# Graph network kernel: the local pass multiplies full fp32 words, and VectorE makes the clamp in front of the inverse root

## What is computed

```python
def _gcn_conv(x, W, b, src, dst, dinv):
    h = x @ W
    norm = dinv[src] * dinv[dst]
    agg = jax.ops.segment_sum(h[src] * norm[:, None], dst, num_segments=x.shape[0])
    return agg + (dinv * dinv)[:, None] * h + b
x = _l2norm(_gcn_conv(node_embedding, W1, b1, ...))          # 128 -> 256
def f(z):
    z1 = _l2norm(_gcn_conv(z, Wf1, bf1, ...))                # 256 -> 256
    return _gcn_conv(z1, Wf2, bf2, ...) + z
k1 = f(x); k2 = f(x + 0.5 * k1); k3 = f(x + 0.5 * k2); k4 = f(x + k3)
x = x + (k1 + 2.0 * k2 + 2.0 * k3 + k4) / 6.0
return _gcn_conv(x, W2, b2, ...)                             # 256 -> 128
x = _layernorm(x + that)
```

## Time and profile before

| | us |
|---|---|
| time before, median of 2 runs | 7419.17 (7414.28 to 7424.07) |
| span of the profiled execution | 7463.9 |
| PE busy in it | 6262.2 (84%) |
| DVE busy | 6114.0 (82%) |
| POOL busy | 4840.9 (65%) |
| ACT busy | 3838.3 (51%) |

### The profile page before, as it was taken

The page is one execution under the profiler, slowest core; times in us unless marked ns, Lnnn a source line. Parts: engine busy times, 40 slices in busy tenths (PEclk is TensorE's granted clock), DMA queues, the critical chain, the costliest instruction groups (busy, mean ns, idle before and its releaser), DMA issues. The chain is left out here.

```text
span 7463.9 us, 156875 instructions
## 1 busy us (share of the span) xinstructions
PE 6262.2 (84%) x37260; PEld 5197.7 (70%) x37260; DVE 6114.0 (82%) x15796; ACT 3838.3 (51%) x10696; POOL 4840.9 (65%) x5469
## 2 busy tenths in 40 slices
PE   7699889899999657989989998999888765877776
PEld 3588888888889436867766676667666554865664
DVE  8588778787888777889879977997799887878887
ACT  6466666666666576733661166116622233654443
POOL 0488888888873576855776577657744565546665
PEclk8799999999999899999999999999999998988998
DMA  0365555554444466879779977997799765543432
GB/s 2 102 165 161 161 160 158 162 161 152 146 145 152 146 190 199 247 257 297 229 223 332 329 226 224 331 327 228 230 385 387 259 186 151 152 138 119 125 123 86
DMA packets 981268, 1483.74 MB, mean 199 GB/s; under 512 B 156967, under 2 KB 450705, under 8 KB 980647
## 3 DMA queue, kind: packets, MB, share of 16 engines
q1 hardware_dynamic: 685479, 922.39, 37.2%
q0 software_dynamic: 141504, 309.42, 16.2%
q10 hardware_dynamic: 153664, 244.12, 9.0%
HBM read 902.58 MB, written 573.11 MB: 198 GB/s over the span
## 5 line engine op out<-in xcount | busy, mean ns | idle before, releaser
L1336 PE MATMUL bank<-c_rows,sums_all 128*128 128x256 f32 (+1 forms) x3920 | 1320.9, 420 | 550.5 <-DVE c_rows L1487 304.3
L751 PE MATMUL bank<-wf_w,c_xt 128*128 128x256 f32 x6272 | 1615.0, 381 | 2.0 <-DVE y L1545 2.0
L1381 ACT ACTIVATE c_xt<-bank 128x512 f32<-128x512 f32 (+1 forms) x980 | 556.8, 568 | 1586.6 <-issue 831.0
L1307 POOL DMA_INDIRECT c_rows<-t_tab,src_pair x784 | 870.2, 1110 | 705.6 <-PE bank L1336 546.2
L1336 PEld LDWEIGHTS bank<-c_rows,sums_all 128*128 128x128 f32 x3920 | 633.9, 194 | 984.7 <-DVE c_rows L1487 478.7
L751 PEld LDWEIGHTS bank<-wf_w,c_xt 128*128 128x128 f32 x6272 | 1133.7, 191 | 127.0 <-ACT c_xt L1381 3.5
L1487 DVE SCALAR_TENSOR_TENSOR c_rows<-bank,carry,c_rows 32x256 f32<-32x256 f32 (+1 forms) x1950 | 913.7, 469 | 274.3 <-PE bank L1336 117.6
L1307 POOL DMA_INDIRECT c_rows<-z_tab,src_pair x784 | 770.7, 983 | 293.3 <-issue 189.5
L1085 DVE TENSOR_TENSOR lx_lo<-bank,lx_hi 128x512 fp32r<-128x512 f32 (+1 forms) x1000 | 658.6, 659 | 260.6 <-ACT lx_hi L1030 217.4
L1030 ACT ACTIVATE lx_hi<-bank 128x512 fp32r<-128x512 f32 (+1 forms) x1000 | 569.4, 572 | 580.4 <-PE bank L999 418.6
L741 PE MATMUL bank<-wf_hi,lx_hi 128*128 128x256 f32 x3200 | 725.0, 309 | 62.7 <-issue 49.4
(11 more groups left out here) (333 smaller groups left out, 14629.2 us busy)
## 6 DMA issues: line engine op xcount, KB each, us to landing
c_z<-z_tab SPq DMA_DIRECT2D x882, 256.0 KB
z_tab<-lz SPq DMA_DIRECT2D x400, 256.0 KB
t_tab<-lt SPq DMA_DIRECT2D x400, 256.0 KB
z_tab<-y ACTq DMA_DIRECT2D x392, 256.0 KB
c_own<-z_tab SPq DMA_DIRECT2D x392, 256.0 KB
t_tab<-y ACTq DMA_DIRECT2D x392, 256.0 KB
c_own<-t_tab SPq DMA_DIRECT2D x392, 256.0 KB
fl_x<-x_tab SPq DMA_DIRECT2D x396, 128.0 KB
```

The source lines that it names most:

```text
L751: last = nc.tensor.matmul(out, x(k), w[:, k, :], start=(k == 0), stop=(k == ks - 1 and not bias))
L1307: pool.indirect_dma_start(out=rows[:, s, i, 0:win], out_offset=None, in_=source, in_offset=bass.IndirectOffsetOnAxis(ap=m["src_i"][:, t:t ...
L1336: nc.tensor.matmul(psum[s % 2][:, i * win:(i + 1) * win], sums[:, j * 2 + i, :], rows[:, s, i, 0:win], start=True, stop=True).then_inc(S[" ...
L1381: nc.scalar.activation(xt[:, s % 2].rearrange("p k n -> p (k n)")[:, 0:n], psum[2 + s % 2][:, 0:n], ACT.Copy).then_inc(S["copied"], 1)
```

## The change

The two fp32r tiles x_hi and x_lo become one fp32 tile xt. `high` becomes `copy` with the same ACT operation and shape; `low` is gone, and with it all waits for it. `multiply` calls `full_product`, which makes one fp32 matmul where there were three fp32r ones: 4 in a mid, end or last step, 2 in a first one; the bias matmul stays in fp32r. The clamp moves from POOL's `invert` to DVE, as the first thing of a turn, for step t-6. The split weights, their tiles and their operations are gone. The sizes, the blocks, the lags of what stays and the indirect DMAs are the same.

```diff
             def _(act):
-                act.wait_ge(S["weights_in"], 64)
-                for n, (name, ks, width, _) in enumerate(parts):
-                    last = nc.scalar.activation(m[name + "_hi"][:, 0:ks, :], m[name + "_w"][:], ACT.Copy)
-                last.then_inc(S["w_hi"], 1)
...
-                for n, (name, ks, width, _) in enumerate(parts):
-                    nc.vector.tensor_tensor(m[name + "_lo"][:, 0:ks, :], m[name + "_w"][:],
-                                            m[name + "_hi"][:, 0:ks, :].bitcast(F32), ALU.subtract)
...
-        x_hi = sb("lx_hi", [P, 4, 2, H2], F32R)
-        x_lo = sb("lx_lo", [P, 4, 2, H2], F32R)
+        xt = sb("lxt", [P, 4, 2, H2])
...
                 def invert(b, q, odd):
                     h = odd * G + group[q]
-                    if normed[q]:
-                        pool.wait_ge(S["squared"], ph.at("squared", b, q))
-                        nc.gpsimd.tensor_scalar(ss[:, h, :], ss[:, h, :], L2_EPS ** 2, None, ALU.max
-                                                ).then_inc(S["clamped"], 1)
-                    elif rooted[q]:
-                        pool.wait_ge(S["chain"], ph.at("chain", b, q))
-                        nc.gpsimd.tensor_scalar(ss[:, h, :], mv[:, h, :, 1], LN_EPS, None, ALU.add
-                                                ).then_inc(S["clamped"], 1)
                     if rooted[q]:
                         pool.wait_ge(S["clamped"], ph.at("clamped", b, q))
...
                     if prev:
-                        pe.wait_ge(S["low"], ph.at("low", *prev))
+                        pe.wait_ge(S["copied"], ph.at("copied", *prev))
...
-                    pe.wait_ge(S["high"], ph.at("high", b, q))
-                    pe.wait_ge(S["low"], ph.at("low", b, q))
+                    pe.wait_ge(S["copied"], ph.at("copied", b, q))
...
-                        last = product(nc, psum[4 + n][:, i * width:(i + 1) * width],
-                                       lambda k: x_hi[:, n, k, i * P:(i + 1) * P],
-                                       lambda k: x_lo[:, n, k, i * P:(i + 1) * P],
-                                       m[w + "_hi"], m[w + "_lo"], ks,
-                                       (m["ones_r"], m["bf2_parts"]) if kind[c] == "end" else None)
+                        last = full_product(nc, psum[4 + n][:, i * width:(i + 1) * width],
+                                            lambda k: xt[:, n, k, i * P:(i + 1) * P], m[w + "_w"], ks,
+                                            (m["ones_r"][:], m["bf2_parts"][:]) if kind[c] == "end" else None)
...
-                def low(b, q, odd):
-                    n = H2 if layer[q] == 0 else 2 * H2
-                    k = bank(b, q)
-                    dve.wait_ge(S["high"], ph.at("high", b, q))
-                    v.tensor_tensor(x_lo[:, k].rearrange("p k n -> p (k n)")[:, 0:n], psum[k][:, 0:n],
-                                    x_hi[:, k].rearrange("p k n -> p (k n)")[:, 0:n].bitcast(F32),
-                                    ALU.subtract).then_inc(S["low"], 1)
+                def clamp(b, q, odd):
+                    h = odd * G + group[q]
+                    if normed[q]:
+                        dve.wait_ge(S["squared"], ph.at("squared", b, q))
+                        v.tensor_scalar(ss[:, h, :], ss[:, h, :], L2_EPS ** 2, None, ALU.max).then_inc(S["clamped"], 1)
+                    elif rooted[q]:
+                        dve.wait_ge(S["chain"], ph.at("chain", b, q))
+                        v.tensor_scalar(ss[:, h, :], mv[:, h, :, 1], LN_EPS, None, ALU.add).then_inc(S["clamped"], 1)
...
-                staggered(dve, blocks, Q, early, [(6, normalise), (1, low), (3, add_rest), (3, take), (0, build)])
+                staggered(dve, blocks, Q, early, [(6, clamp), (6, normalise), (3, add_rest), (3, take), (0, build)])
```

More of the change, by code:

```diff
@@ L266, in gnn_kernel @@
         early("dst_f", [P, TE])
-        for name, ks, width in (("w1", 1, H2), ("wf1", 2, H2), ("wf2", 2, H2), ("w2", 2, D)):
-            early(name + "_hi", [P, ks, width], F32R)
-            early(name + "_lo", [P, ks, width], F32R)
         early("ones_r", [P, P], F32R)
@@ L700, in _ @@
                     sp.dma_start(m[name][:], a[key].partition_broadcast(P)).then_inc(S["biases_in"], 16)
+                sp.wait_ge(S["weights_in"], 64)
                 sp.wait_ge(S["biases_in"], 64)
@@ L713, in _ @@
             def _(dve):
-                dve.wait_ge(S["weights_in"], 64)
-                dve.wait_ge(S["w_hi"], 1)
                 dve.wait_ge(S["biases_in"], 64)
                 nc.vector.tensor_scalar(not_one[:], m["ident"][:, 1:2], -1.0, 1.0, ALU.mult, ALU.add)
-                for n, (name, ks, width, _) in enumerate(parts):
-                    nc.vector.tensor_tensor(m[name + "_lo"][:, 0:ks, :], m[name + "_w"][:],
-                                            m[name + "_hi"][:, 0:ks, :].bitcast(F32), ALU.subtract)
                 nc.vector.tensor_scalar(m["ones_r"][:], m["ident"][:], 0.0, 1.0, ALU.mult, ALU.add)
@@ L733, in _ @@
                                                b_rest[:], ALU.mult, ALU.add)
[L736 to L745, removed]
 def full_product(nc, out, x, w, ks, bias=None):
@@ L818, in local_pass @@
         rates = {
-            "turned": one, "high": one, "low": one, "product": one, "taken": one,
+            "turned": one, "copied": one, "product": one, "taken": one,
             "rest_set": [[0, 0, 0, 0, 1, 0, 1, 0, 3, 1][layer[q]] for q in range(Q)],
@@ L1022, in _, with copy @@
             def _(act):
-                def high(b, q, odd):
+                def copy(b, q, odd):
                     n = H2 if layer[q] == 0 else 2 * H2
@@ L1029, in high @@
                         act.wait_ge(S["product"], ph.at("product", *prev))
-                    nc.scalar.activation(x_hi[:, k].rearrange("p k n -> p (k n)")[:, 0:n], psum[k][:, 0:n],
-                                         ACT.Copy).then_inc(S["high"], 1)
+                    nc.scalar.activation(xt[:, k].rearrange("p k n -> p (k n)")[:, 0:n], psum[k][:, 0:n],
+                                         ACT.Copy).then_inc(S["copied"], 1)
                 def begin_rest(b, q, odd):
@@ L1065, in square @@
                     last.then_inc(S["squared"], 1)
-                staggered(act, blocks, Q, early, [(0, high), (6, scale), (1, begin_rest), (4, square)])
+                staggered(act, blocks, Q, early, [(0, copy), (6, scale), (1, begin_rest), (4, square)])
             @block.vector
```

## The result

| | before | changed |
|---|---|---|
| time, median, us | 7419.17 | 7497.66 (7491.11 to 7504.22) |
| ratio to before | | 1.0106, interval 1.0076 to 1.0135 |
| span of the profiled execution, us | 7463.9 | 7502.5 |
| last power of the local pass, us from the start | 2483.2 | 2550.2 |

The account below looks back on a forecast made before the run. POOL was taken as the bound, PE nearly equal. Blocks with tables 97 us, second stretch 18, split weights 2, first and last half block 4: 121 off 7463.9, 1.62%, so 7299 us; range 7195 to 7375.

Parts of the forecast that it names:

- the rule that speaks against the change: Trainium skill on PE's products: true fp32 takes four passes through the array, so would cost more than the three replaced.
- the prediction's own sum of PE: PE's work per block: 136 matmuls of 256 columns, 16 of 128, 152 transposes, 32 bias matmuls; 49 us.
- The fourth rival: PE's fp32 matmuls take four passes at 0.12 us each, 90 us of PE a block: 7503 us; chance 3%.
- What bounds the kernel before: Local pass, blocks with tables: POOL, with 95% of the stretch, is the bound, PE nearly equal to it.
- Clamps off POOL, net 4.3 us a block, 97 in all: Blocks with tables: 12 or 13 clamps save POOL 0.36 us each, 4.7, less about 0.4 lost in layer 9.
- The round of layer 9: Layer 9: DVE's clamp, POOL's power and DVE's normalise follow in turn, 5.15 us; powers 5.9, 5.1, 3.3, 2.2 us apart.
- The sum of the rest: Outside the blocks with tables: second stretch 18 us, split weights 2, first and last half block 4.
- The second rival: Layers 1 to 8: DVE's clamp ahead of `take` waits for a square and eats the gain; 7395 us, chance 10%.
- The third: PE's clock stays at 1.2 instead of 2.4 GHz through longer gaps: 281 us more, 7698; chance 3%.

Follow-up runs that it names:

- two passes: Kernel before with two fp32r matmuls per product, x_lo by w_hi and `low` left out: 7244.5 us with all clamps on VectorE, 7339.0 with all on GpSimd.
- the three kernels named at the start: Kernel before with all clamps on VectorE (7479.2 us), with only layer 9's left on GpSimd (7402.4), or with the subtraction ahead of normalise (7415.2).
- one pass: Kernel before with one fp32r matmul per product (x_hi by w_hi alone) and the clamp on VectorE: 7246.0 us.

## Why the prediction was wrong

**The step that failed** is "four fp32 ones of 128x256 by the very function that is called now take 0.86 us, 0.215 each". They are two matmuls, 0.43 each. From it followed "PE's work becomes 49 us instead of some 77", and the answer to the rule that speaks against the change, "the trace does not agree in time". It does. PE's pair of steps became 4.57 us. With 0.43 in place of 0.215 the prediction's own sum of PE gives some 80 us a block (136 x 0.43 + 16 x 0.22 + 18), and the trace has 82.6, where 49 were forecast. (The "some 77" for before is what the trace shows; the same terms would give 72.)

The fourth rival, which I gave 3%, had the right cause: 7503 us forecast, 7497.7 measured. That is nearer than its reasoning deserves. It took 0.48 us for a matmul of 0.43, and its block would be pure PE, 90 us with tables and without; the trace has 91.8, since PE still waits in layers 9 and 0, and 84.4. The two errors nearly cancel, which is luck.

**What bounds the kernel before**: right. POOL, with PE close behind. The kernel with two passes and all clamps on POOL had PE and DVE thinned and saved only 1.4 us of a block of 88.8.

**Clamps off POOL, net 4.3 us a block, 97 in all**: right in size where its condition holds, 94.6 between the runs with two passes. Without the condition (PE and DVE thin) the same edit costs 62 us. In the changed kernel, where DVE alone is thin, it is worth nothing (7497.7 and 7498.2).

**The round of layer 9**: right to a tenth of a microsecond, in the changed kernel too, whose powers there are these (in every second block from the seventh on the first gap is 7.4 to 8.1):

```profile
1033.86 0.73 POOL L873 TENSOR_TENSOR linv<-lss,lneg_half 128x2 f32<-128x2 f32 x1
...
1039.64 0.74 POOL L873 TENSOR_TENSOR linv<-lss,lneg_half 128x2 f32<-128x2 f32 x1
...
1044.82 0.71 POOL L873 TENSOR_TENSOR linv<-lss,lneg_half 128x2 f32<-128x2 f32 x1 [1.99 <-DVE lss L1053]
...
1048.14 0.72 POOL L873 TENSOR_TENSOR linv<-lss,lneg_half 128x2 f32<-128x2 f32 x1
...
1050.32 1.38 POOL L873 TENSOR_TENSOR linv<-lss,lneg_half 128x2 f32<-128x2 f32 x2 [0.27 <-DVE lss L1050]
```

Its price was right at two passes (44 us, for 1.8 to 2.0 us in each of 22.5 blocks, 41 to 45) and in the changed kernel (45). I hadn't asked what it would be with three products and `low` kept: 77 us.

**The sum of the rest** was too small: 121 us for the 173 that came when a product costs 0.24. Of the difference, the clamps have nothing (97 and 95). So thinner PE and DVE alone are worth 78 us where I had 24. The trace with two passes and the clamps on POOL places them: the 20 blocks with tables save 29 us, where I had put nothing, and from the first gather behind them to the last power it takes 280 us for 326 (2118.66 to 2398.32, and 2157.47 to 2483.24). Its third block begins 10 us earlier than in the trace of before (371.08 for 381.14), but no earlier than in the three kernels named at the start, so this isn't a gain. The stretch without tables and the two ends, 24 us in the sum, are 46. Why the blocks with tables save anything, with POOL as their bound, no run shows.

**The second rival**, DVE's order eating the gain, had the right place but the wrong layers: in layer 9 and where DVE is full. **The third**, PE's clock, is no danger as a whole, as the run with one pass shows at 0.82. In the run with the clamp alone it fell in layer 9, in blocks that lost 5 us and in blocks that didn't, so that it cost anything there isn't shown.

## What to carry to other kernels

Before a cost per record goes into a sum, count the records of that line against the matmuls the program writes for it; an fp32 matmul left two of them in this trace. When work moves from one engine to another, ask what that engine has to finish before it reaches the moved instruction: here the clamp was cheap (0.16 us for 0.36), but moving all 24 a block behind a `take` cost 62 us in one kernel, gained 95 in another and did nothing in a third, by what else the engines had to do. A block picked out of a trace may be one of two kinds, so lay the same view of its neighbour beside it. Two changes that each cost time may add up to no more than the dearer one, so test the halves before judging either. And look at what one profiled execution has alone before taking it for a cost: that of before was 45 us over the runs.

## What the runs showed of the hardware that was not expected

- One fp32 matmul of 128x256 is two records 0.215 us apart, 0.43 us, against 0.12 us for fp32r: 3.6 times.
- Three fp32r matmuls on rounded parts (0.36 us) are therefore cheaper for PE than one fp32 matmul. Against them stands VectorE's subtraction for the low part, 0.34 to 0.68 us a step.
- The clock granted to PE from 300 to 2200 us was 0.99 in the changed kernel, 0.90 at two passes and 0.82 at one, and the last two took the same time.
